# A decoder layer's cross stage: a bound per chunk, queries projected in chunk 2, copies on ScalarE

## What is computed

```python
def _L0_xattn_ref(query, key, value, mask, Wq, Wk, Wv, Wu, bu):
    scale = DK ** 0.25
    q = einsum('bsd,hdk->bhsk', query, Wq) / scale
    k = einsum('bsd,hdk->bhsk', key, Wk) / scale
    v = einsum('bsd,hdk->bhsk', value, Wv)
    scores = where(mask == 0, -1e9, einsum('bhsk,bhtk->bhst', q, k))
    out = einsum('bhst,bhtk->bhsk', softmax(scores), v)
    return out.transpose(0, 2, 1, 3).reshape(B, S, D) @ Wu + bu

x = x + attention(layernorm(x))                       # per batch
x = x + _L0_xattn_ref(layernorm(x), ctx, ctx, mask, ...)
x = x + experts(layernorm(x))                         # softmax gate, top 2
```

## Time and profile before

| | |
|---|---|
| median of 3 runs | 862.06 us (856.72 to 862.58) |
| the profiled execution | 858.68 us, its span 856.5 us |
| TensorE busy | 749.8 us (88%), mean granted clock 0.941 |
| VectorE, ScalarE, GpSimd busy | 379.4, 397.9, 146.3 us |
| share of the chain that ended last | TensorE 75%, VectorE 13%, transfers 4% |

### The profile page before, as it was taken

One profiled execution on the slowest core, in us unless ns is written; L12 is line 12 of the kernel. 1 busy time (PEld: TensorE's weight loads), 2 busy tenths in 40 slices (PEclk: granted clock), 3 DMA queues, 4 the chain that ended last, 5 costly groups with the idle time before them and its releaser, 6 DMA issues.

```text
span 856.5 us, 17765 instructions
## 1 busy us (share of the span) xinstructions
PE 749.8 (88%) x6649; PEld 444.1 (52%) x6650; DVE 379.4 (44%) x1041; ACT 397.9 (46%) x493; POOL 146.3 (17%) x126
## 2 busy tenths in 40 slices
PE   2997998999999999868878796899999999999830
PEld 1453444456644444425445474566766766766620
DVE  5681220201155454496656642344444444444337
ACT  2556986888889898634433322211211211221123
POOL 5000150010000000200214133143222122122410
PEclk9996998999999999998789888999999999999985
DMA  9689989994417338094499665444444445444443
GB/s 211 158 220 163 299 63 254 227 267 51 56 23 95 46 51 93 3 176 176 72 133 284 197 228 185 126 115 121 109 113 123 118 103 123 120 100 125 79 117 98
DMA packets 94707, 116.15 MB, mean 136 GB/s; under 512 B 14652, under 2 KB 79382, under 8 KB 94612
## 3 DMA queue, kind: packets, MB, share of 16 engines
q1 hardware_dynamic: 87484, 105.78, 54.0%
q0 software_dynamic: 7152, 9.38, 6.6%
HBM read 72.80 MB, written 42.32 MB: 134 GB/s over the span
## 4 chain that ended last, share of the span: by engine, by line
PE 75%; DVE 13%; DMA 4%; issue 3%; ACT 2%; POOL 2%; SPq 1%; DVEq 0%; POOLq 0%; ACTq 0%
PE ps L1734 15%; PE ps L2044 14%; PE ps L2061 14%; PE ps L1711 13%; PE ps L2052 3%; PE ps L1871 2%; PE ps L1693 1%; DMA head_rows<-const_head_rows 1%; PE ps L1940 1%; PE ps L1749 1%; PE ps L1787 1%; PE ps L1910 1%; PE ps L2034 1%; PE ps L1839 1%; DMA sums_by_row<-arena 1%
## 5 line engine op out<-in xcount | busy, mean ns | idle before, releaser
L795 ACT ACTIVATE arena<-ps 128x1024 f32<-128x1024 f32 x256 | 241.8, 1033 | 45.6 <-PE ps L1734 45.1
L1734 PE MATMUL ps<-arena 99*32 99x512 bf16 x2048 | 170.7, 394 | 8.8 <-issue 5.4
L1711 PE MATMUL ps<-arena 128*32 128x256 f32 x2048 | 166.6, 385 | 1.7 <-issue 1.6
L2044 PE MATMUL ps<-arena 128*128 x280 | 129.2, 605 | 0.5 <-ACT arena L901 0.5
L2061 PE MATMUL ps<-arena,xh_tag 128*128 x560 | 126.8, 379 | 1.7 <-DVE xh_tag L1459 1.7
L2061 PEld LDWEIGHTS ps<-arena,xh_tag 128*128 128x128 f32 x560 | 103.7, 190 | 15.0 <-issue 2.4
L901 ACT COPY arena<-ps 128x256 f32<-128x256 f32 x35 | 13.0, 372 | 202.9 <-PE ps L2034 202.9
L713 POOL DMA_INDIRECT sums_by_row<-arena x39 | 60.3, 1547 | 228.4 <-DVE arena L1481 227.2
L1711 PEld LDWEIGHTS ps<-arena 128*32 128x32 f32 x2048 | 70.7, 112 | 52.5 <-issue 6.6
L1454 DVE TENSOR_TENSOR xh_tag<-ps,xh_tag 128x1024 f32<-128x1024 f32 x35 | 42.9, 1225 | 91.6 <-PE ps L2044 91.6
L1734 PEld LDWEIGHTS ps<-arena 99*32 99x32 bf16 x2048 | 43.4, 96 | 75.9 <-ACT arena L795 48.6
(11 more groups left out here) (238 smaller groups left out, 824.0 us busy)
## 6 DMA issues: line engine op xcount, KB each, us to landing
xh_tag<-in_L_ffn_b SPq DMA_DIRECT2D x35, 512.0 KB, 3.7
rows_by_expert<-arena SPq DMA_DIRECT2D x9, 1950.0 KB, 20.4
arena<-in_L_ffn_W SPq DMA_DIRECT2D x16, 1024.0 KB, 13.7
arena<-k_parts SPq DMA_DIRECT2D x48, 128.0 KB
arena<-q_parts SPq DMA_DIRECT2D x48, 128.0 KB
arena<-q_parts SPq DMA_DIRECT2D x24, 256.0 KB, 9.4
q_parts<-arena SPq DMA_DIRECT2D x12, 384.0 KB, 2.9
arena<-rows_by_expert SPq DMA_DIRECT2D x35, 130.0 KB, 2.1
```

What stands on the lines that cost most here:

```text
L795: nc.scalar.activation(probs_of(stage, h), ps[:, 2 * (u % 2):2 * (u % 2) + 2, :].rearrange("p a n -> p (a n)"), ACT.Exp, scale=float(D) ** ...
L1711: last = nc.tensor.matmul(ps[32 * h:32 * h + 32, 4 + half, at:at + 256], v_grp[n % 2][:, kt, h, :], probs_of(stage, h)[:, 256 * part:256 * ...
L1734: last = nc.tensor.matmul(ps[c:c + 32, 2 * (u % 2) + half, :], k_stk[buf][:, h, P * st + c:P * st + c + 32], q_stk[buf][:, h, 512 * half:5 ...
L2044: last = nc.tensor.matmul(ps[:, half, :], xs_t[:, buf, k, :], w1_sb[:, bass.ds(e, 1), k, 512 * half:512 * (half + 1)].squeeze(1), start=(k ...
```

## The change

- **A flag for each chunk of batch 1.** `flags` has four places, and `with_maxima` picks that of the chunk. Where chunk 2's flag is not set, the semaphores of batch 1 that its maxima would have raised are raised without them.
- **Batch 1's second half is projected in chunk 2**, at the places where the first half is projected in chunk 1, with its split, its bound (now in bank 7, between the gate and the last but one turn) and its flag.
- **`leave` moves from VectorE to ScalarE**, one head group behind the exponentials; VectorE's order in chunk 0 changes accordingly.
- **GpSimd's addition for batch 1 moves to VectorE** (`second_shifted`, in chunk 2).
- **The last pair of batch 0** is split behind the bound's sizes and the first copy of the outputs, not ahead of them (`split_pair`).

All engines:

```diff
+FLAG_OF = (1, 1, 2, 3)
...
+        def with_maxima(on, eng, ch, body, counts=()):
+            eng.wait_ge(flag_set, FLAG_OF[ch] + 1)
+            flag = on.alloc_register(f"flag_of_{ch}_{on.engine.name}")
+            on.reg_load(flag, flags[0:1, FLAG_OF[ch]:FLAG_OF[ch] + 1])
+            with eng.If_ne(flag, 0):
+                body()
+            if ch == 2 and counts:
+                with eng.If_eq(flag, 0):
+                    for s, step in counts:
+                        eng.sem_inc(s, step)
```

SyncE, in chunks 2 and 3:

```diff
                 queries_out(NG + ch - 2)
                 sp.wait_ge(s2_ready, 8 * (ch - 1))
                 queries_in(ch)
-            maxima_out(2)
+                if ch == 2:
+                    maxima_out(2)
```

ScalarE:

```diff
+            def leave(n):
+                if n >= 2:
+                    act.wait_ge(o2_tr_done, n - 1)
+                act.wait_ge(pv2_done, n + 1)
+                nc.scalar.copy(o2_tr[:, n % 2, :], ps[:, 4, :]).then_inc(o2_out, 1)
...
+                        if pr == 1 and hg >= 1:
+                            leave(NG * ch + hg - 1)
...
-                        if ch == 1 and (hg, pr) == (1, 1):
-                            second_columns(0)
-                        if ch == 1 and (hg, pr) == (2, 0):
-                            second_queries(0)
-                        if ch == 1 and (hg, pr) == (2, 1):
-                            second_halves(0)
+                        if ch in (1, 2) and (hg, pr) == (1, 1):
+                            second_columns(ch - 1)
+                        if ch in (1, 2) and (hg, pr) == (2, 0):
+                            second_queries(ch - 1)
+                        if ch in (1, 2) and (hg, pr) == (2, 1):
+                            second_halves(ch - 1)
...
-                if ch == 1:
-                    second_columns(1)
-                    second_queries(1)
-                    second_halves(1)
+                leave(NG * ch + NG - 1)
```

VectorE:

```diff
             pair_rows_of(NG - 1)
-            outputs_out(1, NG - 1, lambda: cross_sizes(NG))
+            cross_sizes(0, NG)
+            outputs_out(1, NG - 1, lambda: split_pair(NG - 1))
...
                 if ch == 2:
-                    second_rest(1)
-                    second_sizes(1)
-                    cross_sizes(2)
-                    second_split(1)
                     divide(n - 1)
-                    bound_flag(float(DH) ** -0.5, 2, 4, link)
...
                     root3(ch - 1)
                     divide(n)
                     normalise3(ch - 1)
-                    if ch == 1:
-                        second_rest(0)
-                        second_sizes(0)
-                    leave(n + 1)
-                    if ch == 1:
-                        second_split(0)
+                    if ch < 3:
+                        second_rest(ch - 1)
+                        second_sizes(ch - 1)
+                        cross_sizes(ch - 1, ch)
+                        second_split(ch - 1)
                     divide(n + 1)
-                    leave(n + 2)
                     choose(ch - 1)
+                    if ch < 3:
+                        bound_flag(float(DH) ** -0.5, ch + 1, 7, link)
+                    if ch == 2:
+                        second_shifted()
                     divide(n + 2)
-                leave(n + 3)
```

TensorE:

```diff
                 if ch == 2:
                     turn2(n - 1)
                     outputs(1)
-                    pe.wait_ge(o2_out, n)
-                    head_bounds(2, 4)
                     add_product(1)
...
-                if ch == 1:
-                    second_columns(0)
+                if ch in (1, 2):
+                    second_columns(ch - 1)
                 scores2(ch, 2, 0)
                 turn2(n)
-                if ch == 1:
-                    second_queries(0)
+                if ch in (1, 2):
+                    second_queries(ch - 1)
...
                 if ch >= 1:
                     gates(ch - 1)
+                if ch in (1, 2):
+                    head_bounds(ch + 1, 7)
                 turn2(n + 2)
-                if ch == 1:
-                    second_columns(1)
                 values2(n + 3)
-                if ch == 1:
-                    second_queries(1)
```

VectorE's order in chunk 0, before and after:

```diff
                     second_root(1e-3)
-                    leave(n)
+                    divide(n)
                     second_scaled()
-                    divide(n)
-                    leave(n + 1)
+                    divide(n + 1)
                     second_added()
+                    divide(n + 2)
                     second_moments(x_sb)
-                    divide(n + 1)
-                    leave(n + 2)
                     second_root(1e-5)
                     second_normalised()
-                    divide(n + 2)
```

More of the change, by code:

```diff
@@ L353, in queries_written, with needed @@
             eng.wait_ge(q2_out[n % 2], 16 * KC * (n // 2 + 1))
-        def needed(on, eng, which, at=0):
+        def needed(on, eng, which):
             eng.wait_ge(flag_set, which + 1)
-            flag = on.alloc_register(f"flag_{which}_{at}_{on.engine.name}")
+            flag = on.alloc_register(f"flag_{which}_{on.engine.name}")
             on.reg_load(flag, flags[0:1, which:which + 1])
             return eng.If_ne(flag, 0)
+        def with_maxima(on, eng, ch, body, counts=()):
[8 more added lines that the diff above has]
+                        eng.sem_inc(s, step)
         @block.sync
@@ L523, in maxima_out, with body @@
             def maxima_out(ch):
-                with needed(nc.sync, sp, 1 + ch // 2, ch % 2):
+                def body():
                     sp.wait_ge(max2_split[ch // 2], ch % 2 + 1)
@@ L689, in _ @@
                         last.then_inc(x_shifted, 1)
[L691 to L697, removed]
+            pool.wait_ge(xh_ready, NT + CP)
+            nc.gpsimd.tensor_tensor(x_sb[:, 0:CP, :], x_sb[:, 0:CP, :], xbu_sb.unsqueeze(1).to_broadcast([P, CP, D]),
+                                    ALU.add).then_inc(x_shifted, 1)
             pool.wait_ge(xs_zero, 16 * 9)
@@ L858, in _ @@
                     turned_outputs(1)
-                with needed(nc.scalar, act, 1 + b, i):
-                    act.wait_ge(shift2_out[b], 48 * (i + 1))
+                with_maxima(nc.scalar, act, ch, lambda: act.wait_ge(shift2_out[b], 48 * (i + 1)))
                 for hg in range(NG):
@@ L1129, in _, with cross_sizes @@
                 group_outputs(0, g)
-            def cross_sizes(n):
-                dve.wait_ge(q2_ready, NG + 1)
-                link(nc.vector.tensor_reduce(size[:, :, 0], sizes[:, :, 0, 0:n], AX.X, ALU.max))
+            def cross_sizes(first, end):
+                link(nc.vector.tensor_reduce(size[:, :, 0], sizes[:, :, 0, first:end], AX.X, ALU.max))
                 link(nc.vector.tensor_copy(size[:, :, 1], k2_size[:, :]))
@@ L1182, in pair_rows_of, with split_pair @@
                 pair_q = ps[:, 7, :].rearrange("p (m n) -> p m n", m=KC)
[L1183 removed]
+                link(nc.vector.tensor_reduce(sizes[:, :, 0, g:g + 1], pair_q, AX.X, ALU.max, apply_absolute_value=True))
+            def split_pair(g):
+                pair_q = ps[:, 7, :].rearrange("p (m n) -> p m n", m=KC)
                 part0, part1, part2 = (q2_split[:, c, :, 256 * (g % 2):256 * (g % 2 + 1)] for c in range(3))
@@ L1205, in cross_maxima, with body @@
                 b, i = divmod(ch, 2)
-                with needed(nc.vector, dve, 1 + b, i):
+                def body():
                     linked = link_on(dve_max2[b], i * (2 * CHUNK + 4))
@@ L1361, in place, with second_shifted @@
                 nc.vector.tensor_copy(seen_bf[:, :], seen[:, :]).then_inc(seen_ready, 1)
+            def second_shifted():
+                dve.wait_ge(second_ready, CP)
+                nc.vector.tensor_tensor(x_sb[:, CP:NT, :], x_sb[:, CP:NT, :], xbu_sb.unsqueeze(1).to_broadcast([P, CP, D]),
+                                        ALU.add).then_inc(x_shifted, 1)
             dve.wait_ge(seen_ready, 1)
@@ L1931, in second_columns @@
                 pe.wait_ge(second_ready, CHUNK * (i + 1))
-                free = ((gate_read, i), (gate_read, i)) if i else ((x2_added, 1), (x2_added, 2))
+                free = ((x2_added, 3), (rank_read, 1)) if i else ((x2_added, 1), (x2_added, 2))
                 turn_rows(CP + CHUNK * i, free, x2_ps)
@@ L1955, in _, with general @@
                 pe.wait_ge(q2_in[i], 16 * 6 * (b + 1))
-                with needed(nc.tensor, pe, 1 + b, i):
+                def general():
                     if ch == 0:
```

23 lines of the change are left out of this document (12 added, 11 removed).

## The result

The kernel after takes 868.33 us (median of 20 runs, 860.43 to 874.88), the one before in the same series 860.58 (20 runs, 853.64 to 868.50). The ratio is 1.0084, with an interval of 1.0060 to 1.0108: slower by 7.2 us. The profiled execution of after has a span of 871.2 us at a mean granted clock of 0.926 (before: 856.5 and 0.941). That is 14.7 us more, and it isn't all the change's: in this execution the last turn of the self attention stands at 367.00, 1.66 us later than in the earlier trace rows; the part behind chunk 3's outputs took 370.5 us where it took 366.6; the cross stage between them is 9.2 us longer. In the ten profiled executions here that computed the same number of expert tiles (35 of the program's 39), the last part takes 366.6 to 371.4 us, whatever the edit.

A forecast was written before the change was run, and what follows sets the result against it. No engine is full, so the order of waits sets the time. +10.8 us at chunk 3's start, 0 behind it, 1.3 off for the clock make +9.5: 868.2 or 871.6, forecast 870 us, range 857 to 878.

The forecast's parts named there:

- Split of the last pair: End of batch 0's self attention: TensorE's last turn still waits for the second copy; gain 0, bound -0.3 to +0.3 us.
- Chunk 0's outputs: Copies moved to ScalarE and one wait gone: outputs turned at about 390.3 us instead of 394.17.
- Chunk 1's split: First half's split on VectorE ends at 412.1 us instead of 417.3, with 3.9 us of GpSimd contention gone.
- Chunk 2's scores: First scores wait for their queries and start at 432.5 us, 9.4 us earlier than 441.9.
- Chunk 2's split: Second half's split, now in chunk 2, ends 18 us after the first scores, at 450.5 us.
- Round trip: Queries from split through memory write and six reads until scores can begin, chunks 2 and 3: 20.1 us.
- Chunk 3's scores: First scores wait for the second trip through memory: 470.6 us instead of 459.84, 10.8 us later.
- Behind it: Chunk 3's first scores to its outputs: 30.1 us, bounds 26.5 and 31, no net change, slow clock offsetting gains.
- Rival 1: Queries' trip through memory too short to be seen at chunks 2 and 3: -7 us (chance 0.07) or -13 (0.10).
- the point of balance: Length of the queries' trip through memory at which chunk 3's scores start as early as before: 14.9 us.
- Rival 2: Waits as forecast, but split and clock come out so well that time hardly changes: +0 to +3 us, chance 0.09.
- Rival 3: ScalarE's copies behind its exponentials hold back TensorE's turns in every chunk: at most 0.7 us each, +3; chance counted within forecast's 0.74.

The follow-up runs named there:

- e5: The kernel before with only the last pair of batch 0 split behind the bound's sizes and the first copy: 859.34 us, ratio 0.9979.
- e3: The kernel before with only the copies of values on ScalarE and VectorE's changed order in chunk 0: 855.77 us, ratio 0.9942.
- e6: The kernel after with copies back on VectorE and batch 1's addition back on GpSimd, leaving the moved projection and late split: 874.94 us, ratio 1.0159.
- e7: The kernel after with each of six query reads writing 32 rows by 8 heads, queries misplaced, other experts chosen: 868.56 us, ratio 1.0090.
- e2: The kernel after with chunk 3's reads taking chunk 2's queries, so no wait for its own (wrong results): 854.14 us, ratio 0.9930.
- e1: The kernel before with every part of the change except the moved second-half projection and the per-chunk flag: 854.22 us, ratio 0.9921.
- e4: The kernel before with only batch 1's addition moved from GpSimd to VectorE, behind the flag of batch 1: 855.37 us, ratio 0.9941.
- e8: The kernel after with queries stored by head, six writes, and three reads of 48, 32 and 16 rows: 867.32 us, ratio 1.0083.
- e9: The kernel after with queries stored by head, six writes, and six reads of 32 rows, results correct: 867.29 us, ratio 1.0040.

## Why the prediction was right

To set the clocks of after beside those predicted, 1.66 us are taken off (last turn of the self attention 367.00 against 365.34).

- **Split of the last pair: 0 predicted,** with a bound of 0.3. Nearly right: from the start of the last pair's reduction on VectorE to the last turn there are 5.76 us in after and in e5, and 5.36 in before, so 0.4 us are lost ahead of the stage. The last turn waits 3.31 us in one piece for the second copy, where before 2.50 us ahead of the bound's matmul and 0.36 behind it stood in its place. e5's row of the table is 0.6 to 2.4 us worse and its ratio 0.2% better, so no effect on the time is found. I said that chunk 1's scores were covered by 4 us. They were not: TensorE waited 2.81 us for those reads at 386.44. It cost nothing, because the outputs behind them waited for VectorE still.
- **Chunk 0's outputs: 390.3 predicted,** 390.6 measured. The copies and the one wait gave the 3.9 us; e3 shows that they alone do.
- **Chunk 1's split: end at 412.1 predicted,** write issued at 412.7. The 3.9 us of contention are right as a term: 5.15 to 5.21 us in four kernels with GpSimd's addition beside the subtractions (before, e3, e5, e6), 1.29 to 1.30 in the seven without it. The sum itself names a copy that goes from VectorE (0.6) and does not take it off. From chunk 0's outputs to the end of the split after takes 22.0 us, 2.8 more than before does without the contention (23.1 - 3.9); I had added 1.1 for the copy on ScalarE and 1.5 for the clock, and these are not told apart.
- **Chunk 2's scores: 432.5 predicted,** 433.2 measured. The wait in front was not the 5 us that I had: TensorE was not free at 427 but at 431.0 (432.6 less 1.66), since from the split's end chunk 1's rest took 18.3 us and not 15, its add alone 6.45 at a granted clock of 0.50 to 0.53 until 432. The scores came when forecast because the queries were later still.
- **Chunk 2's split: end at 450.5,** write issued at 450.2; the 18 us for the sequence behind the first scores came to 16.9 (434.90 to 451.83).
- **Round trip: 20.1 us.** To the last landing the chain gives 19.4 for chunk 2 and 19.7 for chunk 3 (414.34 to 433.75, 451.83 to 471.50), to the scores 20.6 and 20.3.
- **Chunk 3's scores: 470.6 predicted,** 470.5 measured, 10.7 us later than before. TensorE idled 13.94 us, about the 14 forecast.
- **Behind it: 30.1 us, no change, predicted;** 28.6 measured (472.17 to 500.73). The first scores of chunk 3 follow each other at 0.43 us where the later ones take 0.22: the granted clock is 0.50 (1.2 GHz) from 472 to 476 and 1.00 from 477, as forecast. At chunks 1 and 2 it is 1.00 at the first scores and 0.50 by 388 and 436, and at chunk 2 it is back at 1.00 by 439. The term was 1.5 us too high, all of it ahead of chunk 2's outputs, which came 4.2 us behind the scores where I had 5.8. That the 1.3 which I took off the sum for a clock that recovers early is nearly as much is in part luck; so the stage comes to +9.2 against +9.5.
- **From the stage to the time.** 860.58 + 7.2 to 7.75 is 868 us against 870. I had used 862.06 as the median of before, which 20 runs put 1.5 lower, and the change itself is 2 us smaller than the stage of one execution says. No run here splits that further. The forecast gave 0.46 to a loss of over 1% and 0.44 to a change within 1%; the measured 0.84%, with its interval of 0.60 to 1.08, lies mostly on the second side.

Rival 1, a round trip too short to be seen, falls with the two waits of 16.7 us. In e7, with 14 to 15 us, chunk 3's outputs are back where before has them, though its scores still start 2.2 us late: the point of balance of 14.9 took TensorE to be free at 427. The rival's larger claim, that with neither wait the change would win 13 us, was not run; e2, which lacks only the wait at chunk 3, stands at -6, and two things speak against the rest. Shorter reads can't bring chunk 2 forward by more than its wait of 2.27 us (3.49 in e2), and the work that I had named for the case without the wait, the flag, the addition and the divisions behind it, then shows. Rival 2 had the waits right and the sum at 0 to +3; measured is +7. Rival 3, ScalarE's copies as a cost, is wrong by e3: the kernel with them wins 5 us.

What I did not see is what e1 shows: three of the four parts together are a gain of 0.8%, so that the forecast of the sum hid a better kernel. **e1 is the fastest kernel of this study that computes the layer,** 0.9921 of before and 0.984 of after; its lead over e3 and e4 lies within the intervals, but its chunk 3 outputs are 3 us or more ahead of theirs in the table.

## What to carry to other kernels

When a projection is moved later, look at when its last consumer is due and at the whole way there, writes and reads through memory included: here 17 us of work and 20 us of transfers stand between chunk 2's start and chunk 3's, which before were 18 us apart. Price each part of a mixed change by itself, since a gain of 0.8% and a loss of 1.6% look like a small loss. And when something is put in front of a write whose landing is awaited, count the issue time on its queue too: six small writes gave back 3 to 4 of the 5.6 us that faster reads had won.

## What the runs showed of the hardware

**The rate of a read depends on how many rows of SBUF it writes.** The same 1.5 MB, in pieces of 1 KB, with the transfer engines' busy share over 1 in each case; each row is a stretch of 3 us of chunk 3's reads, of after, e7, e8 and e9 in turn (last number: GB/s). For e8 a stretch of chunk 2's reads stands ahead of it, and behind it the time from issue to landing of its three reads, of 48, 32 and 16 rows, which land in this order.

```profile
460.00:463.00 3.00, 0.00 (x0) 0.00 (x0) 1.57 (x3) 0.00 (x0) 0.00 (x0) 0.50 1.17 114
```

```profile
453.00:456.00 3.00, 0.72 (x4) 0.00 (x0) 2.79 (x10) 0.59 (x1) 0.00 (x0) 0.50 1.11 226
```

```profile
416.00:419.00 3.00, 2.33 (x10) 1.83 (x9) 0.00 (x0) 1.17 (x2) 0.00 (x0) 0.50 1.17 123
454.00:457.00 3.00, 0.00 (x0) 0.00 (x0) 0.42 (x1) 0.00 (x0) 0.00 (x0) 0.50 1.01 164
DMA to landing us min/median/max: 8.5/11.0/12.5
```

```profile
454.00:457.00 3.00, 0.00 (x0) 0.00 (x0) 0.00 (x0) 0.00 (x0) 0.00 (x0) 0.50 1.15 191
```

16 rows have 114 GB/s and 32 rows 191 in e9. The 226 of e7 holds the start of its reads, with 293 in the first us; from 454 to 457 it has 192. The 164 of e8 is a start too: over 455 to 460, all within the transfer of 48 rows, the trace has 134, and 123 in the middle of the one of chunk 2. From the landings (issues at 452.62, 452.98 and 453.55) the 512 KB of 32 rows took 2.9 us, about 180 GB/s, and the 256 KB of 16 rows 2.1, about 125. So a transfer of 48 rows is slower than one of 32. A busy share of 1.17 at 114 GB/s is thus no sign that the engines could do no more. The Trainium skill ("SBUF — State Buffer", Door 1: The DMA port swizzle) states it: a transfer's rate goes by how many of 16 ports its partitions reach, 0 to 15 reach four (104 GB/s measured there with 1 MB), 0 to 31 eight (189). The trace agrees, with 114 and 191. By that page's port map 48 partitions load half of their eight ports twice, an estimate of three quarters of the rate of 32, which is 142 GB/s at the page's 189; the trace has 123 to 134. The prediction took its round trip from the rows of before, so it had the rate right without its cause. The table of rates by size that it weighed against them (the Trainium skill, "DMA: Bandwidth & Descriptors", Bandwidth) is headed as measured with 128 partitions, and these reads write 16.

**Two operands in SBUF beside GpSimd.** VectorE's two subtractions of 512 elements with both operands in SBUF took 5.15 to 5.21 us while GpSimd added 2048 elements, in four kernels, and 1.29 to 1.30 without it, in seven. The addition itself takes 4.52 us on GpSimd and 2.27 on VectorE:

```profile
458.71 2.27 DVE L1385 TENSOR_TENSOR x_sb<-x_sb,rows_sb 128x2048 f32<-128x2048 f32 x1
```

So moving it to the engine that it held up was worth it, 0.59% by e4, although VectorE then does 2.27 us of it itself.
